# Top-2 routing in a fused conv, attention and expert kernel: one root by a power on GpSimd, and another order of the values, weights and choices

## The reference

```python
h = jnp.tanh(q + k + bh)                       # attention, 32 keys per token
a = jax.nn.softmax(e - 10000.0 * (1.0 - band), axis=-1)
v = jnp.einsum('bts,bsf->btf', a, x)           # the "values"
t = t + v                                      # tokens after attention
t = t + _L1_ffn_ref(_ln_t(t), ...)             # layer norm, then the experts:
    logits = xt @ Wr + br
    probs = jax.nn.softmax(logits, axis=-1)
    top_p, top_idx = jax.lax.top_k(probs, 2)
    weights = top_p / top_p.sum(axis=-1, keepdims=True)
    xn = (xt - mu) * jax.lax.rsqrt(var + LN_EPS)
    out = sum over the two chosen experts e of weights * (gelu(xe[e] @ W1[e] + b1) @ W2[e] + b2)
```

## Time and profile before

| | us |
|---|---|
| median of three runs | 1007.38 |
| lowest, highest | 1003.4, 1008.6 |
| the profiled execution | 1005.29 |
| its span in the profile | 1003.5 |
| routing: first operation of `experts` on DVE to the end of the last indirect DMA on POOL | 725.08 to 843.14 |
| sixteen indirect DMAs of a group on POOL | 19.9 to 20.7 |

### The profile page before, as it was taken

The page is one execution under the profiler, slowest core; times in us unless marked ns, Lnnn a source line. Parts: engine busy times, 40 slices in busy tenths (PEclk is TensorE's granted clock), DMA queues, the critical chain, the costliest instruction groups (busy, mean ns, idle before and its releaser), DMA issues. The chain is left out here.

```text
span 1003.5 us, 24055 instructions
## 1 busy us (share of the span) xinstructions
PE 754.5 (75%) x7837; PEld 474.5 (47%) x7837; DVE 721.0 (72%) x1821; ACT 615.7 (61%) x1382; POOL 587.0 (58%) x760
## 2 busy tenths in 40 slices
PE   2766888888888888888888859965576521999960
PEld 2453444445444544444444524431165421899950
DVE  2576778778788788887877861569777771677757
ACT  2565777777777777777777723228633320988840
POOL 0045686776777767768677649920006674466660
PEclk9996999999999999999999969977855555999995
DMA  9009999990000000000000015014001112233318
GB/s 227 1 2 173 157 204 159 20 5 0 0 0 0 0 0 0 0 0 0 0 0 0 0 26 145 0 44 143 2 2 38 48 51 62 65 95 89 92 54 251
DMA packets 109052, 54.07 MB, mean 54 GB/s; under 512 B 42688, under 2 KB 100824, under 8 KB 109008
## 3 DMA queue, kind: packets, MB, share of 16 engines
q1 hardware_dynamic: 102624, 43.34, 28.5%
q0 software_dynamic: 4544, 9.38, 2.9%
q10 hardware_dynamic: 1840, 0.79, 0.5%
HBM read 21.49 MB, written 29.44 MB: 51 GB/s over the span
## 5 line engine op out<-in xcount | busy, mean ns | idle before, releaser
L528 DVE SCALAR_TENSOR_TENSOR l_m<-l_m,l_eta,lp_g 128x256 f32<-128x256 f32 x512 | 219.3, 475 | 46.4 <-PE lp_g L641 26.0
L383 POOL TENSOR_TENSOR s_w<-l_kw,l_m 128x512 f32<-128x512 f32 x192 | 238.4, 1281 | 12.2 <-DVE l_m L528 12.2
L476 ACT ACTIVATE l_kw<-s_w,l_keep_lr 128x256 f32<-128x256 f32 x384 | 171.2, 506 | 0.0
L1333 POOL DMA_INDIRECT f_yg<-f_yr,f_xmeta x78 | 78.4, 1005 | 54.5 <-DVE f_yr L1663 41.7
L1328 POOL DMA_INDIRECT f_xg<-f_xrow,f_place x64 | 63.2, 988 | 54.3 <-DVE f_place L1559 35.7
L469 ACT COPY l_wt<-lp_b 128x512 f32<-128x512 f32 x96 | 56.5, 588 | 27.7 <-PE lp_b L634 27.7
L1308 ACT ACTIVATE f_hh<-fp_v,f_bcol 128x256 f32<-128x256 f32 x156 | 61.3, 477 | 12.9 <-DVE f_hs_lo L1654 8.5
L388 POOL TENSOR_TENSOR l_kw<-s_w,l_keep 128x512 f32<-128x512 f32 x64 | 65.1, 1035 | 0.0
L634 PE MATMUL lp_b<-s_cst,s_w 128*128 128x128 f32 x384 | 62.2, 285 | 2.2 <-ACT s_w L515 1.3
L634 PEld LDWEIGHTS lp_b<-s_cst,s_w 128*128 128x128 f32 x384 | 43.3, 142 | 32.2 <-ACT l_wt L469 13.8
L1428 PE MATMUL fp_v<-f_xf,s_w_hi 128*128 128x256 bf16 x312 | 55.5, 280 | 1.4 <-DVE f_xmeta L1643 1.0
(11 more groups left out here) (320 smaller groups left out, 1991.3 us busy)
## 6 DMA issues: line engine op xcount, KB each, us to landing
f_xg<-s_pad SPq DMA_DIRECT2D x1, 17280.0 KB, 107.0
f_xt<-f_xg SPq DMA_DIRECT2D x39, 130.0 KB
r_w<-in_L_ffn_W_dram SPq DMA_DIRECT2D x16, 256.0 KB, 3.2
s_w<-f_yg SPq DMA_DIRECT2D x16, 256.0 KB, 3.7
xs<-in_x_dram SPq DMA_DIRECT2D x8, 256.0 KB, 7.6
t_w<-in_L_ffn_W_dram SPq DMA_DIRECT2D x8, 256.0 KB
out_dram<-s_x SPq DMA_DIRECT2D x8, 256.0 KB, 3.0
s_xsh<-s_xl SPq DMA_DIRECT2D x4, 448.0 KB, 3.5
```

What stands on the lines that cost most here:

```text
L383: nc.gpsimd.tensor_tensor(W[k][:, half(h), :], KW[k][:, half(h), :], M[k][:, half(h), :], ALU.add).then_inc(w_ready[k], 1)
L476: m = nc.scalar.mul(KW[k][:, b, :], W[k][:, b, :], keep_lr[:, b:b + 1])
L528: i = nc.vector.scalar_tensor_tensor(out=M[k][:, b, :], in0=M[k][:, b, :], scalar=eta[:, b:b + 1], in1=ps_g[b][:, 0:256], op0=ALU.mult, op ...
L1333: nc.gpsimd.indirect_dma_start(sb["yg"][:, :], bass.IndirectOffsetOnAxis(ap=xmeta[:, j, a, 0:1].bitcast(mybir.dt.int32), axis=0), yr[j % R ...
```

## The change

The change has three parts.

1. The first group's root. POOL fills a buffer `f_mhalf` with -0.5 and raises `f_sq` of group 0 to that power, straight into `f_rd`. ACT takes the root, and DVE the reciprocal, for groups 1 to 3 only. The product `s2`, so far `sr * rd`, becomes `sq * rd * rd'` in two operations, for every group.
2. The end of the softmax for tiles 2 to 7 moves behind `normed(0)` on DVE, and `valued(1)` follows `valued(0)` directly.
3. `routed(g)` is cut in two: `routed(g)` ends at `f_both`, and `placed(g)` has the rest. The loops are written in another order on DVE, PE and ACT.

```diff
@@ ACT @@
                 for g in range(GR):
+                    if g >= 1:
+                        roots(g)
+                    rows(g)
+                    features(g)
                     if 2 * g + 2 < NTB:
                         turned_weights(2 * g + 2)
-                    roots(g)
-                    rows(g)
-                    features(g)
+                    odds(g)
+                    second(g)
                     if 2 * g + 3 < NTB:
                         turned_weights(2 * g + 3)
-                    second(g)
-                    odds(g)
@@ POOL, ahead of the indirect DMAs @@
+                nc.gpsimd.memset(mhalf[:, :, :], -0.5).then_inc(id_ready, 1)
+                pool.wait_ge(id_ready, 3)
+                pool.wait_ge(nrm, 3)
+                nc.gpsimd.tensor_tensor(rd[:, :, :], sq[:, :, :], mhalf[:, :, :], ALU.pow).then_inc(nrm, 1)
@@ PE @@
                 for g in range(GR):
+                    router(g)
                     if 2 * g + 2 < NTB:
                         weights(2 * g + 2)
+                    counts(g)
+                    if 2 * g + 2 < NTB:
                         values(2 * g + 2)
-                    router(g)
-                    if 2 * g + 3 < NTB:
                         weights(2 * g + 3)
                         values(2 * g + 3)
-                    counts(g)
@@ DVE: normed, routed and the order @@
-                    dve.wait_ge(sq_ready, g + 1)
-                    nc.vector.reciprocal(rd[:, :, :], sr[:, :, :]).then_inc(nrm, 1)
+                    if g >= 1:
+                        dve.wait_ge(sq_ready, g)
+                        nc.vector.reciprocal(rd[:, :, :], sr[:, :, :]).then_inc(nrm, 1)
                     dve.wait_ge(nrm, 4 * g + 4)
...
-                    link(nc.vector.tensor_tensor(s2[:, :], sr[:, 0, :], rd[:, 1, :], ALU.mult))
+                    link(nc.vector.tensor_tensor(s2[:, :], sq[:, 0, :], rd[:, 0, :], ALU.mult))
+                    link(nc.vector.tensor_tensor(s2[:, :], s2[:, :], rd[:, 1, :], ALU.mult))
...
                     nc.vector.tensor_tensor(both[:, :, :].rearrange("p e n -> p n e"), one[:, :, :], two[:, :, :], ALU.add).then_inc(count_ready, 1)
+
+                def placed(g):
                     dve.wait_ge(ex_ready, g + 1)
...
                 valued(0)
-                dve.wait_ge(soft, 10)
-                nc.vector.reciprocal(m_late, m_late).then_inc(soft, 1)
-                dve.wait_ge(soft, 11)
-                nc.vector.tensor_tensor(er, er, bc, ALU.mult).then_inc(soft, 1)
-                dve.wait_ge(soft, 12)
-                masked(2)
                 valued(1)
                 for g in range(GR):
                     spread(g)
-                    if 2 * g + 3 < NTB:
+                    normed(g)
+                    if g == 0:
...
+                        nc.vector.reciprocal(m_late, m_late).then_inc(soft, 1)
...
+                        nc.vector.tensor_tensor(er, er, bc, ALU.mult).then_inc(soft, 1)
...
+                    if 2 * g + 2 < NTB:
+                        masked(2 * g + 2)
+                    remainder(g)
+                    routed(g)
+                    if 2 * g + 2 < NTB:
                         masked(2 * g + 3)
-                    normed(g)
+                    placed(g)
                     if 2 * g + 2 < NTB:
                         valued(2 * g + 2)
-                    remainder(g)
-                    routed(g)
-                    if 2 * g + 4 < NTB:
-                        masked(2 * g + 4)
-                    if 2 * g + 3 < NTB:
                         valued(2 * g + 3)
```

More of the change, by code:

```diff
@@ L1154, in experts @@
         var, s2 = (buf(n, [128, GT]) for n in ("var", "s2"))
-        sq, sr, rd = (buf(n, [128, 2, GT]) for n in ("sq", "sr", "rd"))
+        sq, sr, rd, mhalf = (buf(n, [128, 2, GT]) for n in ("sq", "sr", "rd", "mhalf"))
         xn = [buf(f"xn{i}", [128, GT, 128]) for i in range(2)]
@@ L1376, in counts @@
                     pe.wait_ge(count_ready, g + 1)
-                    pe.wait_ge(id_ready, 2)
+                    pe.wait_ge(id_ready, 3)
                     flat = both[:, :, :].rearrange("p e n -> p (e n)")
@@ L1585, in _ @@
                     spread(g)
-                    if 2 * g + 3 < NTB:
+                    normed(g)
+                    if g == 0:
+                        dve.wait_ge(soft, 10)
+                        nc.vector.reciprocal(m_late, m_late).then_inc(soft, 1)
+                        dve.wait_ge(soft, 11)
+                        nc.vector.tensor_tensor(er, er, bc, ALU.mult).then_inc(soft, 1)
+                        dve.wait_ge(soft, 12)
+                    if 2 * g + 2 < NTB:
[3 more added lines that the diff above has]
+                    if 2 * g + 2 < NTB:
                         masked(2 * g + 3)
-                    normed(g)
+                    placed(g)
                     if 2 * g + 2 < NTB:
                         valued(2 * g + 2)
-                    remainder(g)
-                    routed(g)
-                    if 2 * g + 4 < NTB:
-                        masked(2 * g + 4)
-                    if 2 * g + 3 < NTB:
                         valued(2 * g + 3)
```

## The result

The changed kernel took 1009.19 us (median of eight runs, lowest 1008.25) against 1003.48 us of the kernel before in eight runs. The ratio is 1.0057, 95% interval 1.0035 to 1.0078: slower by 5.7 us, just over the 5 us that can be told from no change. One of the changed kernel's eight runs took 2312.66 us and is left out of the ratio; without it the median is 1008.98 us. The time lies inside the forecast range; the forecast 1013.2 was 4 us above it. The profiled execution of the changed kernel took 1008.25 us, span 1006.4.

A forecast was written before the change was run, and what follows sets the result against it. The routing's wait chain up to POOL's last indirect DMA bounds the kernel. First group 1.3 us plus three periods 6.8 us, less 1.07 us slack, gave 7.0 us later: 1012.3 by the profiled time, put at 1013.2; range 1006 to 1016.5.

The forecast's parts named there:

- What bounds: Routing: the wait chain ends in POOL's indirect DMAs; when the last lands decides when the expert part starts.
- the slack of 1.07 us: POOL's fourth group: its places were finished 1.07 us earlier than POOL needed them, so that much delay is absorbed.
- `valued(1)` earlier: First group on DVE: without softmax's end and one mask before it, it starts at 735.25 instead of 735.99 us.
- The power: First group on POOL: takes 3.5 us, going by columns; normed tokens start 1.3 us later.
- The Trainium skill's price per element: Power on POOL: 2.6 cycles per element would make twelve more columns cost 0.03 us; the forecast rejected this.
- The period: Routing loop, choice to choice: 24.0 us against 21.8, bound by PE's chain; three periods cost 6.8 us more.
- the chain: Loop from choice through counts, first values, weights, ACT's copy, second values and router to the next choice: 24.0 us.
- The sum: End of routing: group 3's choice 8.1 us later, POOL's last DMA 7.0 us later after slack; forecast 1013.2 us.
- The short power: Rival, first group on POOL: power takes 1.04 us, a fixed cost; end 4.5 us later, 1010.8 us; chance 0.20.
- The rising clock: Rival, PE in the loop: each second values 1.23 us shorter, up to 3.7 us in all; chance 0.20.
- The clock that stays up: Rival, PE through all groups: high clock saves 18 us or so per period; 1002.2 or 1004 us; chance 0.04.

The follow-up runs named there:

- experiment 1: Changed kernel with the first group's root put back on ACT and DVE (square root, reciprocal); ratio to the kernel before 1.0031.
- experiment 3: Changed kernel with the values of tile 2g+2 moved ahead of the counts on PE; ratio to the kernel before 1.0064.
- experiment 2: Changed kernel with the mask of tile 2g+3 moved ahead of the choice on DVE; ratio to the kernel before 1.0060.
- experiment 7: Kernel before with ACT's exponential ahead of the long copy, PE's counts ahead of tile 2g+3's values, DVE's tile 2g+4 mask in the router's wait; ratio 0.9981.
- experiment 4: Changed kernel with the values of tile 2g+2 ahead of the counts on PE and the product buffer in two halves; ratio to the kernel before 1.0093.

## Why the prediction was right

- *What bounds.* Right. Each experiment's time followed its length to within 1.1 us; the way from the last DMA to the first expert product stayed at 5.5 to 5.9 us. The last choice came 7.1 us later and the last DMA 6.05: the slack of 1.07 us was used up as forecast.
- *`valued(1)` earlier.* Right: it started 10.20 us behind POOL's first operation instead of 10.95, by 0.75 us (0.74 forecast).
- *The power.* Right in kind: DVE stood still for it. The term was mis-sized: 2.90 us instead of 3.5. A line through the two widths has 0.41 us and 0.155 us per column, so by it most of the 2.90 goes by columns, with a larger fixed part than I took. The first choice came 24.12 us behind POOL's first operation instead of 23.40: 0.7 us later (1.3 forecast). Against the best root for that place it cost 2.5 us (experiment 1), which I had not worked out. Nor was the root's table load wholly covered in the kernel before: DVE waited 0.33 us for it.
- *The Trainium skill's price per element.* By the 2.6 cycles per element that the Trainium skill gives ("GPSIMD Engine Reference", section 3.1) 128x16 would have taken about 1.06 us, an estimate from its 1.2 GHz on top of the 1.035 us of the earlier trace rows. The trace shows 2.90; the figure does not carry over to a power.
- *The period.* Right: 23.9 us (24.0 forecast), the three together 71.69 us against 65.29, 6.4 more (6.8 forecast; three times the chain's 24.0 is 72.0 and not 72.1, so 6.7 by its own terms). No term of the chain was off by more than 0.13 us, so this was not luck. The idle time of DVE at the second values was 2.1 to 2.2 us (1.7 forecast), and POOL's before groups 1 to 3 was 2.29, 3.55 and 3.19 us (3.8 forecast; the first is shorter because POOL's first sixteen DMAs began 0.7 us later behind their places than the others and took 0.7 us longer). One thing was missing in the reasoning: with the values ahead of the counts the single product buffer would have held the chain at the same place (experiment 3).
- *The sum.* 6.05 us in the profile, 5.7 in the runs, 7.0 forecast: 0.6 of the difference from the power and 0.4 from the period. The larger part of the 4 us by which the forecast time was too high is its base: the three runs shown had a median of 1007.38, eight have 1003.48, and I moved from the profiled 1005.29 towards the first.
- *The rivals.* The short power is refuted. The rising clock did not come in the loop of the changed kernel's one profile. It came in one group of experiment 2, worth 1.9 us there, and in two of experiment 7, off the chain. PE's order alone does not decide it: experiment 2 has the changed kernel's. The clock that stays up was not seen.

## What to carry to other kernels

Work filled into a wait is free only if nothing on the chain waits for what comes behind it: take the distance between two passes of the loop through every engine, not the idle times of one. Moving two dependent steps into one gap puts them in series; a single buffer between them counts as much as the order. An operation moved to an idle engine has to be shorter than what it replaces where it stands, not where it stood; here a root that takes 0.57 us once its table is loaded, as it would have been, was replaced by 2.9 us for which the vector engine stood still.

## What the runs showed of the hardware that I had not expected

- A power on GpSimd takes longer with more columns: 1.035 us for 128x4, 2.90 us for 128x16 in each of the five profiles that have it.
- Four products of 32 rows each, into four banks, took 0.81 us together; two such products, into two banks, took 0.80 us (changed kernel and experiment 4, both at a granted clock of 0.50). So halving their number per turn saved nothing.
- A table load (`ACT_TABLE_LOAD`) runs ahead of its instruction's wait: in experiment 1 it began at 732.96, 4.2 us before the root that it serves.
- The same order of products met the low clock in one execution and the high one in another: the values of tile 1 ran at the high clock in the changed kernel's profile and at the low one in those of experiments 2 and 3, a difference of 1.4 us where the kernels do not differ.
